# A decoder in one program: another order of instructions at the end of a cross attention and at the ends of the Performer's half layers

## The reference

```python
x = x + local_attention(layernorm(x))             # A: 16 heads, window 32
x = x + topk_attention(layernorm(x), ctx)         # B: 154 keys, the 32 best of each row
x = x + fp4_ffn(layernorm(x))                     # C: weights and inputs rounded to FP4
x = x + performer(layernorm(x))                   # D: 6 layers, below
x = x + cross_attention(layernorm(x), ctx)        # E: 16 heads
x = x + six_local_attention_and_ffn_layers(layernorm(x))   # F
```

```python
# B, for each batch
q = xn @ Wq.T + bq; k = ctx @ Wk.T + bk; v = ctx @ Wv.T + bv
s = q @ k.T / sqrt(128)                     # 512 x 154, all but the top 32 of a row masked
out = softmax(s) @ v @ Wo.T + bo
# D, for each of 6 layers; phi(t) = [exp(t@om - |t|^2/2), exp(-t@om - |t|^2/2)]
q, k, v = o @ Wq + bq, o @ Wk + bk, o @ Wv + bv
a = causal_linear_attention(phi(q), phi(k), v)       # chunks of 128 tokens
h1 = layernorm(o + a @ Wo + bo) * g1 + be1
o  = layernorm(h1 + relu(h1 @ W1 + bf1) @ W2 + bf2) * g2 + be2
```

## Time and profile before

| | us |
|---|---|
| median of 3 runs | 1667.17 |
| lowest and highest of them | 1661.9, 1668.22 |
| the profiled execution, its own time | 1669.83 |
| its span in the trace | 1667.9 |
| end of stage B and start of C in the trace, from about | 175 to 214 |
| stage D in the trace, about | 263 to 660 |

### The profile page before, as it was taken

The page is one execution under the profiler, slowest core; times in us unless marked ns, Lnnn a source line. Parts: engine busy times, 40 slices in busy tenths (PEclk is TensorE's granted clock), DMA queues, the critical chain, the costliest instruction groups (busy, mean ns, idle before and its releaser), DMA issues.

```text
span 1667.9 us, 37573 instructions
## 1 busy us (share of the span) xinstructions
PE 1531.1 (92%) x15357; PEld 788.0 (47%) x15357; DVE 1170.8 (70%) x2014; ACT 922.0 (55%) x1626; POOL 623.8 (37%) x578
## 2 busy tenths in 40 slices
PE   7787668999999999889999999999999999999996
PEld 2545434545555554333535455453545545363543
DVE  5786575657666665346777878687787877778783
ACT  2435432453445344345667767666776767676673
POOL 5462000010001000104565656555564655556461
PEclk9899677999999999889999999999999999999998
DMA  7143210000000000203142423313242331324120
GB/s 244 41 129 137 95 27 1 8 22 1 22 6 17 22 1 1 97 1 117 22 133 68 138 86 90 129 36 132 69 137 73 103 125 40 125 77 137 57 82 14
DMA packets 52393, 119.38 MB, mean 72 GB/s; under 512 B 15488, under 2 KB 20352, under 8 KB 50816
## 3 DMA queue, kind: packets, MB, share of 16 engines
q1 hardware_dynamic: 52224, 116.99, 21.5%
HBM read 37.52 MB, written 0.52 MB: 23 GB/s over the span
## 4 chain that ended last, share of the span: by engine, by line
PE 65%; DVE 16%; ACT 11%; issue 4%; DMA 2%; POOL 2%; SPq 0%; DVEq 0%; ACTq 0%; POOLq 0%
PE ps L436 5%; PE ps L426 5%; PE ps L292 4%; PE ps L274 4%; PE ps L390 3%; PE ps L284 3%; PE ps L1699 3%; PE ps L407 3%; PE ps L1645 3%; PE ps L1703 2%; ACT big L558 2%; PE ps L1665 2%; DVE nm L676 2%; DVE big L628 2%; ACT big L570 2%
## 5 line engine op out<-in xcount | busy, mean ns | idle before, releaser
L727 POOL TENSOR_TENSOR big<-big 128x512 f32<-128x512 f32 x112 | 144.2, 1288 | 282.3 <-DMA big<-big 281.8
L736 POOL TENSOR_TENSOR big<-big,nm 128x384 f32<-128x384 f32 x224 | 185.1, 847 | 157.0 <-DVE nm L669 157.0
L627 DVE TENSOR_TENSOR big<-ps,big 128x512 f32<-128x512 f32 x224 | 153.8, 686 | 65.9 <-ACT sq L504 40.6
L2059 POOL TENSOR_TENSOR big<-big 128x512 f32<-128x512 f32 x24 | 31.2, 1324 | 415.7 <-ACT big L1834 415.7
L1973 DVE TENSOR_TENSOR big<-ps,fix 128x512 f32<-128x512 f32 x192 | 119.2, 683 | 55.3 <-PE ps L1645 54.9
L558 ACT ACTIVATE big<-big 128x384 f32<-128x384 f32 x224 | 109.3, 523 | 86.3 <-DVE big L679 84.1
L628 DVE TENSOR_TENSOR big<-ps,big 128x512 f32<-128x512 f32 x224 | 152.5, 681 | 0.0
L728 POOL TENSOR_TENSOR big<-big 128x512 f32<-128x512 f32 x112 | 146.2, 1305 | 0.0
L426 PE MATMUL ps<-big 128*64 128x64 f32 x3584 | 131.2, 227 | 12.8 <-ACT big L570 12.8
L426 PEld LDWEIGHTS ps<-big 128*64 128x64 f32 x3584 | 116.6, 140 | 52.7 <-ACT big L570 34.5
L676 DVE TENSOR_REDUCE nm<-ps 128x4 f32<-128x384 f32 x224 | 112.5, 544 | 30.4 <-PE ps L390 27.8
(11 more groups left out here) (307 smaller groups left out, 2833.1 us busy)
## 6 DMA issues: line engine op xcount, KB each, us to landing
big<-big SPq DMA_DIRECT2D x224, 256.0 KB, 2.4
big<-big SPq DMA_DIRECT2D x112, 128.0 KB, 2.4
big<-in_F_w SPq DMA_DIRECT2D x18, 512.0 KB, 4.0
big<-in_zero SPq DMA_DIRECT2D x8, 1088.0 KB, 12.6
big<-big SPq DMA_DIRECT2D x84, 64.0 KB, 2.0
big<-in_D_w SPq DMA_DIRECT2D x12, 256.0 KB, 3.1
big<-in_F_wo SPq DMA_DIRECT2D x6, 512.0 KB, 3.7
big<-in_F_w SPq DMA_DIRECT2D x6, 341.0 KB, 3.3
```

The source lines that it names most:

```text
L627: dve.tensor_tensor(tmp[:, i, w, :], ps[:, k, :], tb[:, 2 * w, :], ALU.mult).then_inc(*part.mark((key, b, p, 0)))
L736: pool.tensor_tensor(v, v, nm[:, p % 3, 16 + 4 * h:20 + 4 * h].unsqueeze(2).to_broadcast([128, 4, KW]), ALU.mult)\
```

## The change

Two places change, in the order of the instructions alone. No operation is added or taken away.

1. **End of B, start of C.** On PE, the loop over tiles no longer holds the weight transposes. `b_out_pe` of batch 0 moves from ahead of tile 6 to ahead of tile 7's transpose. In C, each of the three groups of weight transposes stands in one of the gaps of the second norm C1: ahead of its mean, between mean and variance, and after it. They use banks 4, 5 and 6 in place of 0, 1 and 5. ACT's copies follow likewise, and `b_inv_act` of batch 0 comes right after tile 3. On DVE, `b_norm_dve` of batch 0 stands after tile 6 in place of tile 5, and `out_dve` after tile 7 in place of tile 6.
2. **Ends of the halves of D.** On PE, q, k and v of the next half are written ahead of the numerators of the last chunk; in half 0 v comes right after q and k. On DVE, their bias additions come ahead of the division `d_a_dve`. `d_om_dve` is split: its first operation (`d_bqk_dve`) stays at the end of the layer, its second moves behind the division.

```diff
 def b_pe(pe):
-            for n in range(TILES + 1):
-                if n == TILES - 2:
+            for n in range(TILES):
+                if n == TILES - 1:
                     b_out_pe(pe, 0)
-                if n == TILES - 1:
+                    b_values_pe(pe, n - 1)
                     norm_mean_pe(pe, "C1", 0, 4, x[:, cols(0)], (x_new.at(("B", 0)),))
...
-                if n == NT:
-                    c_w_pe(pe)
+            norm_var_pe(pe, "C1", 0, 4)
+            b_values_pe(pe, TILES - 1)
             c_xn_pe(pe, 0)
             b_out_pe(pe, 1)
...
 def b_act(act):
                 if n == NT:
-                    c_w_act(act)
+                    b_inv_act(act, 0)
+            norm_sq_act(act, "C1", 0, 4)
+            b_turn_act(act, TILES - 1)
...
 def b_dve(dve):
-                if n == TILES - 3:
+                if n == TILES - 2:
                     b_norm_dve(dve, 0)
-                if n == TILES - 2:
-                    out_dve(dve, "B", 0, Bb[:, 3:4], B_Y[0])
+            out_dve(dve, "B", 0, Bb[:, 3:4], B_Y[0])
...
-        C_W = (0, 1, 5)
+        C_W = (4, 5, 6)
...
 def c_pe(pe):
-            norm_pe(pe, "C1", 1, 7, x[:, cols(1)], (x_new.at(("B", 1)),))
+            c_w_pe(pe, 0)
+            norm_mean_pe(pe, "C1", 1, 7, x[:, cols(1)], (x_new.at(("B", 1)),))
+            c_w_pe(pe, 1)
+            norm_var_pe(pe, "C1", 1, 7)
+            c_w_pe(pe, 2)
             c_xn_pe(pe, 1)
...
 def d_pe_half(pe, h):
             d_den_pe(pe, *hd)
+            if nx:
+                d_qk_pe(pe, *nx)
+                d_v_pe(pe, *nx)
             d_num_pe(pe, *hd, 3)
...
 def d_dve_half(dve, h):
+            d_qk_dve(dve, *hd)
+            d_v_dve(dve, *hd)
             if tl:
                 d_a_dve(dve, *tl)
-            if hd:
-                d_qk_dve(dve, *hd)
+            if hd[1] == 0 and hd[0] > 0:
+                d_om_dve(dve, hd[0])
```

More of the change, by code:

```diff
@@ L1018, in b_act @@
             norm_act(act, "B1", 1, 7, 0)
-            for n in range(TILES + 1):
-                if n == NT + 1:
-                    b_inv_act(act, 0)
-                if n == TILES - 2:
+            for n in range(TILES):
+                if n == TILES - 1:
                     b_bias_act(act, 0)
[L1024 to L1027, removed]
+                    b_turn_act(act, n - 1)
+                b_exp_act(act, n)
                 if n == 0:
@@ new lines, in c_w_pe @@
+        def c_w_pe(pe, j):
+            off, k = 24 * j, C_W[j]
+            if j == 0:
+                pe.wait_ge(*q4_w.at("w"))
+            take(pe, k)
+            for ch in range(3):
+                m = min(128, I0 - 128 * ch)
+                if j < 2:
+                    last = pe.transpose(ps[:, k, 128 * ch:128 * ch + m],
+                                        Cw[0:m, off + 8 * ch:off + 8 * ch + 8, :].rearrange("p a b -> p (a b)"), ident[0:m, 0:m])
+                else:
+                    last = pe.transpose(ps[0:m, k, 128 * ch:128 * ch + 128],
+                                        Cw[:, off + 8 * ch:off + 8 * ch + m // FB, :].rearrange("p a b -> p (a b)"), ident[:, :])
+            last.then_inc(*full[k].mark(("C", "w", j)))
@@ new lines, in c_w_act @@
+        def c_w_act(act, j):
+            k = C_W[j]
+            act.wait_ge(*full[k].at(("C", "w", j)))
+            if j < 2:
+                act.activation((gT, uT)[j], ps[:, k, 0:I0], ACT.Copy).then_inc(*turned4.mark(("w", j)))
+            else:
+                step(act, act_step, act.activation(dT[:, 0:2, :], ps[:, k, 0:256].rearrange("p (a b) -> p a b", a=2), ACT.Copy))
+                act.activation(dT[0:96, 2, :], ps[0:96, k, 256:384], ACT.Copy).then_inc(*turned4.mark(("w", 2)))
+            read(act, k, turned4, ("w", j))
@@ L1211, in c_act @@
         def c_act(act):
-            norm_act(act, "C1", 1, 7, 0)
+            c_w_act(act, 0)
+            norm_sq_act(act, "C1", 1, 7)
+            c_w_act(act, 1)
+            norm_root_act(act, "C1", 1, 7, 0)
+            c_w_act(act, 2)
             for b in range(B):
@@ L1762, in d_pe_half @@
                 d_up_pe(pe, *tl, 1)
[L1763 to L1764 removed]
+            else:
+                d0_var_pe(pe)
+            d_scores_pe(pe, *hd, 0)
             if tl:
@@ L2024, in d_dve_half @@
                 d_centre_dve(dve, "D1", *tl, 4, "wo", 0)
[L2025 removed]
+            else:
                 norm_sub_dve(dve, "D0", 1, 4, x[:, cols(1)])
[L2027 to L2031 removed]
+            if hd[1] == 0:
+                d_wo_dve(dve, hd[0])
+            d_scan_dve(dve, *hd, 0)
             if tl:
                 d_scale_norm_dve(dve, "D1", *tl)
[L2034 to L2042 removed]
+            d_scan_dve(dve, *hd, 1)
+            d_mask_dve(dve, *hd, 0)
+            if not tl:
+                d0_mul_dve(dve)
+            d_sum_dve(dve, *hd, 0)
+            d_state_dve(dve, *hd)
+            d_mask_dve(dve, *hd, 1)
+            d_sum_dve(dve, *hd, 1)
             if tl:
                 d_centre_dve(dve, "D2", *tl, 7, "f2", 1)
[L2045 to L2046 removed]
+            d_mask_dve(dve, *hd, 2)
             if tl:
                 d_scale_norm_dve(dve, "D2", *tl)
[L2049 to L2052 removed]
+            d_mask_dve(dve, *hd, 3)
+            if hd[1] == 1 and hd[0] + 1 < LAYERS:
+                d_bqk_dve(dve, hd[0] + 1)
         def d_pool(pool):
```

80 lines of the change are left out of this document (24 added, 56 removed).

## The result

| | before | after |
|---|---|---|
| median, us | 1667.32 (6 runs) | 1655.77 (6 runs) |
| lowest and highest | 1661.9, 1669.16 | 1652.86, 1658.95 |
| profiled execution, its own time | 1669.83 | 1653.17 |
| its span | 1667.9 | 1651.2 |

The ratio of the times is 0.9941 with a 95% interval of 0.9924 to 0.9959: 9.9 us faster, 7 to 13. The two profiled executions lie 16.7 us apart, more than the ratio gives, so a difference between two single traces is read by stretches here and not as a whole.

The account below looks back on a forecast made before the run. In D PE itself was the bound, so only its idle time could go; at the end of B a chain of handovers was. 5.9 + 3.2 = 9.1 us off the median 1667.2 gave 1658.1, range 1652 to 1664.

Parts of the forecast that it names:

- The wait goes at 10 ends ... 6.4 - 5 x 0.1 = 5.9 us: Stage D: PE's wait for DVE's masks, 6.4 us, vanishes at halves 1 to 10, less 0.1 at layer ends.
- L1680 then takes 0.86 ... since two such products take 1.72: Replay of half 3 in D: residual product keeps its duration in the new order; features start 0.6 to 0.7 us earlier.
- Rival 2: D's wait only moves to L1683 or the variance, 0.3 to 0.5 an end; 5.2 in all, or 1662; chance 0.13.
- 0.1 us of new wait there for the layer ends: D's layer ends: PE waits 0.1 us for DVE's division before L1683; nothing at other ends.
- The centring, covered by 0.3: D: k features cover DVE's centring and ACT's square by 0.3 us; if not, variance slips at most 0.3 a half.
- B: 3.2 predicted: End of stage B: rounding of batch 0 starts at 196.4 in place of 199.60, 3.2 us earlier.
- the transposes off the chain: End of B: weight transposes and copies take the chain from 176.83 to 179.48; moving them frees 2.65 us.
- L948 a tile later: End of B: output product moves behind a tile, to 184.05 from 184.75, which eats most of the 2.6 us.
- both clocks for mean and variance: End of B: half clock taken for the replay, 3.2 us; mean, variance and values at full clock would give 5.2.
- Transposes in C1's gaps for nothing: Norm C1: three transpose groups of 0.6 us fit the gaps and cost nothing; without that cover, 1.8 in all.
- The clock of C1 stays at half: Norm C1: transposes do not raise PE's clock; if they did, the sum would be some 1.5 us larger.
- rivals 3 and 4: Clock: half 0 at half clock, up to 11 us more, chance 0.04; or rises in C or half 0, 1653-1656, chance 0.14.

Follow-up runs that it names:

- part2: Only the change in stage D, with the end of B and start of C as in the kernel before; 0.9969 of the time before, 5.2 us faster.
- warm: Changed kernel plus two matmuls of 512 columns, results overwritten, in the gaps of norm C1; 0.9938 of the time before, 10.3 us faster.
- best: resid_fill plus batch 0's output product one tile earlier and warm's two added matmuls; 0.9928 of the time before, 12.0 us faster.
- part1: Only the change at the end of B and start of C, stage D as before; 0.9964 of the time before, 6.0 us faster.
- resid_fill: B and C as changed; D in the old order, with only the residual product moved into the mask wait; 0.9946 of the time before, 9.0 us faster.

## Why the prediction came out right

I said 9.1 us and 1658.1; measured were 9.9 and 7.2 us. The total holds by luck as much as by the mechanism: D gave 2.9 us less than its term, B about 2 more.

- **"The wait goes at 10 ends ... 6.4 - 5 x 0.1 = 5.9 us": the wait went, the size was wrong.** 3.0 us came back. The step that failed is the replay of PE behind it: "L1680 then takes 0.86 ... since two such products take 1.72" and q, k straight behind the denominators at 391.22. I moved products with the durations that they had behind neighbours of their own tile shape. The new order has two more seams, 0.35 us at every end, and at the end of half 0 there was no wait to pay for them. Each pair of halves became 0.63 us shorter (65.97 to 65.34), where I had said 1.2. Rival 2 had the size, 0.3 to 0.5 an end, by the wrong mechanism: no idle time shows at L1686, and at the variance once in the whole of D.
- **"0.1 us of new wait there for the layer ends"**: right in size. The division ends 0.15 before L1686 starts, too late for its load to be hidden: 0.09 at each of the five.
- **The centring, covered by 0.3**: the wait for the square appears once in 290 to 650 (0.7). It holds.
- **B: 3.2 predicted, about 5 measured, by two errors that partly cancel.** B1 to rounding took 44.2 us before (45.7 in part2) and takes 39.6 in the mean of the ten traces with moved transposes. Of it the transposes off the chain: 2.65 predicted, 2.5 to 2.9 measured. L948 a tile later, as said. Inversion to rounding, which I had going from 20.12 to 19.5, is 18.4 in the mean of the changed kernels. First, I had named both clocks for mean and variance and taken the slower. The variance takes 1.14 in every kernel with the new tile order, full clock, against 1.72 before; the mean takes 0.88 here and 0.88 to 1.23 in the others. PE idles 1.31 us ahead of that variance in all of them; before, it idled 1.94 for tile 7. Second, I put the rounding right behind the product L1056. The earlier trace rows have the transposes L1158 between them, 1.06 us from the end of L1056 to the rounding, and it is 1.32 in the changed kernel. With them my replay at half clock gives 2.1 us and not 3.2. With single traces this stretch is good to about 2 us.
- **Transposes in C1's gaps for nothing**: round to round 13.32 before, 13.31 after. Right.
- **The clock of C1 stays at half**: right for the variance, 2.07 or 2.08 in every kernel but warm and best, and warm shows what it was worth, 1 us and not 1.5, since the mean is covered by DVE.
- **Half 0 of D**, rivals 3 and 4 (the stretch here is longer than the prediction's, which starts at 274.44): it took 2.3 us less in the changed kernel's trace, but part1, resid_fill and best, with the old order there, have 27.0, 25.1 and 28.9, and part2 and the changed kernel 25.1 and 26.5. Its length goes with the granted clock, in either order. I can't say which gap brings the clock down, nor what part of any kernel's time this is.

By the traces the change is about 5 in B and 3.0 in D's ends, 8 us. That lies in both intervals; the other 2 of the first comparison are well within the spread of half 0 and of stages E and F.

## What to carry to other kernels

When work is moved into a wait on PE, price the seams too: each product that comes to stand behind another shape of tile, or whose operand comes just before it starts, loads its weights in the open. Here a seam more cost 0.2 us and a late operand 0.09, and they are paid also where there was no wait to fill. Fill the wait with the smallest piece that covers it, in the place where it makes the fewest seams. And when PE's order moves a producer ahead, its consumer on the other engine must move ahead as well: with the division first this change loses 7.7 us in D.

## What the runs showed of the hardware

- A float32 product of 512 columns takes 0.86 us to its successor when both loads are hidden (L1680 in before), 0.97 when its own is bare (L1683 in the changed kernel), and 1.05 when its own is bare and its successor has another tile shape (L1684 in resid_fill).
- A weight load is started 0.43 us ahead, under the product in front, where the tile shape stays the same, and not at all ahead where the shape changes: 149 places of the first kind, ten of them L1686 with its late operand, and 149 of the second in the traces before and after, in D from 290 to 640 us.
- PE can be busy and still be granted half speed: in best the clock is 0.50 from 275 to 280 with PE busy 5.00 of 5 us, while two added products bring the full clock in warm, though PE is then busy only 2.38 of 5 us.
- The same order of D's half 0 takes from 25.1 to 28.9 us in different kernels, but 26.52 and 26.55 in two profiles of one. That does not make the clock a property of the program: the same two profiles differ by 3.4 us at the end of B, where one has 0.91 and the other 1.71 for the values of tile 3.
